# Node stages of a graph network: each close of a pass joined with the next pass's sources, and edge records laid out by partition

## The reference

```python
x = _layernorm(x + L0(x, src, dst, edge_type_16, edge_weight, ...))   # three layers
x = _layernorm(x + L1(x, edge_index, ...))
x = _layernorm(x + L2(x, edge_index, edge_attr_16, ...))
x = _layernorm(x + L3(x, node_vec, edge_weight, edge_attr_64, edge_index, ...))  # two convolutions
```

```python
ht = jnp.einsum('nd,rdo->nro', h, W_rel[l])
h_rel = segment_sum(ht[src, etype], dst) + h @ W_loop[l] + b_rel[l]
h_gat = segment_sum(softmax_over_dst(leaky_relu(el[src] + er[dst])) * z[src], dst) + b_gat[l]
hc = jnp.concatenate([h_rel, h_gat], axis=1) @ W_fuse + b_fuse      # layer 0: times a sigmoid gate
h = relu(hc)
```

## Time and profile before

| | us |
|---|---|
| median of 3 runs (lowest to highest) | 12328.44 (12322.66 to 12332.82) |
| the profiled execution | 12328.02 |
| its span, first to last instruction | 12326.2 |
| busy in it: PE / DVE / POOL / ACT | 8220.5 / 9081.5 / 6770.4 / 3431.0 |
| close and sources of L0 layer 1 together | 502.2 |
| close and sources of L0 layer 2 together | 433.0 |
| last close of L0 and sources of L1 | 375.1 |
| close of L1 and sources of L2 | 363.0 |
| close of L2 and first convolution's sources | 292.9 |
| first convolution's close, second's sources | 140.8 |
| sources of L0 layer 0 / last close | 327.0 / 99.5 |
| reading of the edge records | 203.0 |

### The profile page before, as it was taken

The page is one execution under the profiler, slowest core; times in us unless marked ns, Lnnn a source line. Parts: engine busy times, 40 slices in busy tenths (PEclk is TensorE's granted clock), DMA queues, the critical chain, the costliest instruction groups (busy, mean ns, idle before and its releaser), DMA issues. The chain is left out here.

```text
span 12326.2 us, 169288 instructions
## 1 busy us (share of the span) xinstructions
PE 8220.5 (67%) x50988; PEld 6605.6 (54%) x50988; DVE 9081.5 (74%) x15379; ACT 3431.0 (28%) x7929; POOL 6770.4 (55%) x7047
## 2 busy tenths in 40 slices
PE   3555067887678876788745778437773587858874
PEld 3444035665446654466634666425552577757774
DVE  8666547987469884589865777558887688858886
ACT  0111033333233332333312555313332111101111
POOL 2777106775037770277713777317773377727773
PEclk8555588887788887888866888757776789969996
DMA  4333674444464444644433888502222477747775
GB/s 188 108 110 108 142 305 140 107 108 81 171 226 107 108 105 134 262 107 108 107 40 123 267 269 268 130 26 56 55 56 26 146 262 265 262 111 263 262 264 134
DMA packets 825743, 1884.52 MB, mean 153 GB/s; under 512 B 378601, under 2 KB 437430, under 8 KB 785512
## 3 DMA queue, kind: packets, MB, share of 16 engines
q0 software_dynamic: 306624, 795.04, 26.0%
q1 hardware_dynamic: 518312, 1079.56, 24.5%
HBM read 1284.84 MB, written 589.18 MB: 152 GB/s over the span
## 5 line engine op out<-in xcount | busy, mean ns | idle before, releaser
L974 POOL DMA_INDIRECT h<-table,edges_ring x3552 | 3360.3, 946 | 1135.1 <-issue 1034.8
L974 POOL DMA_INDIRECT edges_rows<-table,edges_ring x1944 | 1859.4, 956 | 599.7 <-issue 578.1
L1149 PE MATMUL bank<-h,edges_onehot 128*128 128x260 f32 (+1 forms) x5312 | 1579.1, 457 | 176.4 <-DVE h L1306 130.2
L1149 PEld LDWEIGHTS bank<-h,edges_onehot 128*128 128x128 f32 x5312 | 1176.6, 253 | 470.1 <-DVE h L1306 234.7
L2434 POOL DMA_INDIRECT rec<-dst,slots x782 | 842.1, 1077 | 433.0 <-issue 414.4
L1260 DVE TENSOR_TENSOR_SCAN bank<-edges_fresh,edges_top,bank 4x1024 f32<-4x1024 bf16 x440 | 1026.2, 2332 | 3.3 <-PE bank L1124 3.3
L1267 DVE TENSOR_TENSOR_SCAN edges_top<-edges_fresh,bank 4x1024 f32<-4x1024 bf16 x440 | 995.0, 2261 | 0.8 <-issue 0.5
L1124 PE MATMUL bank<-ident,edges_score 128*4 128x128 f32 x3520 | 645.3, 345 | 485.4 <-DVE edges_score L1300 484.0
L962 POOL COPY edges_ring<-rel_idx 128x64 uint32<-128x64 uint32 (+1 forms) x42 | 10.3, 244 | 1611.9 <-POOLq L155 1611.8
L974 POOL DMA_INDIRECT acc<-table,edges_ring x664 | 682.4, 1028 | 247.5 <-issue 184.9
L1488 PE MATMUL bank<-edges_w_e,edge_score 128*128 128x128 f32 x3520 | 787.2, 311 | 0.0
(11 more groups left out here) (416 smaller groups left out, 19111.7 us busy)
## 6 DMA issues: line engine op xcount, KB each, us to landing
table<-x SPq DMA_DIRECT2D x154, 1040.0 KB, 8.0
edge_score<-edge_feat SPq DMA_DIRECT2D x220, 512.0 KB
edges_onehot<-onehot_d SPq DMA_DIRECT2D x220, 512.0 KB, 3.7
table<-h SPq DMA_DIRECT2D x77, 1040.0 KB, 7.9
table<-source_typed_rows SPq DMA_DIRECT2D x63, 1040.0 KB, 8.1
h<-table,edges_ring POOLq DMA_INDIRECT x3552
onehot_d<-edges_onehot SPq DMA_DIRECT2D x110, 512.0 KB, 3.6
flip_d<-edges_onehotT SPq DMA_DIRECT2D x110, 512.0 KB
```

Of the source, the lines that this page charges most:

```text
L974: pool.indirect_dma_start(out=rows[r][:, j, :], out_offset=None, in_=table, in_offset=bass.IndirectOffsetOnAxis(ap=ring[:, s * ST + j:s * ...
L1149: ins = pe.matmul(sum_b[k % 3], onehot[s][:, j, :], rows[s][:, j, A0:W], start=j == k * GT, stop=j == (k + 1) * GT - 1)
```

## The change

Every close is joined with the sources that follow it, in one stage with one list per engine; six stages replace twelve (the first sources stage and the last close stand alone), and their steps are written out instead of looped.

`relational_turn(layer)` is sources of an L0 layer, with the close of the layer before it in front. The work on step t+1 that comes before its typed rows is cut in slots 0 to 6, and slot j stands behind bin j of step t on PE, ACT and DVE. PE transposes straight from `acc`, `gat` and `h`; `cur` and `rel` are gone; the transposed tile and `z` have two buffers. `acc` is cleared step by step.

```diff
+    close, gated = layer > 0, layer == 1
...
+                def ahead(n, slot):        # PE
+                    if slot == 0 and close:
+                        hold(pe, loop_kept, n)
+                        turn(lambda j: g.acc[:, bin_at(n, j), 0:D])
+                    if slot == 1 and close:
...
+                        product(pe, g, 1, [(relT, w_fuse[:, 0, :]), (gatT, w_fuse[:, 1, :])], fuse_made)
...
+                    if slot == 5:
...
+                        product(pe, g, 1, [(curT[n % 2], w_z[:, :])], z_made)
+                        product(pe, g, 0, [(curT[n % 2], w_loop[:, :])], loop_made)
...
+                for slot in range(NB):
+                    ahead(0, slot)
+                for t in range(NSTEPS):
+                    for j in range(NB):
+                        typed_rows(t, j)
+                        if t + 1 < NSTEPS:
+                            ahead(t + 1, j)
...
+                    if slot == 6:          # DVE
+                        c.link(v.memset(g.acc[:, bins, D:D + ZW], 0.0))
```

`relational_to_gated` joins the last close of L0 with the sources of L1, `gated_to_attention` the close of L1 with the sources of L2 (its steps run from the last to the first), `attention_to_conv` the close of L2 with the first convolution's sources, `conv_to_conv` the two convolutions. Their DVE lists, one iteration each (function names of the new code):

```diff
+                for i in range(NSTEPS + 1):       # relational_to_gated, DVE
...
+                        attention(i)
...
+                        projected(i - 1)
...
+                        old_nodes(i)
...
+                        hidden(i - 1)
...
+                        keep_nodes(i)
...
+                        end_rows(i - 1)
...
+                for i in range(NSTEPS + 2):       # gated_to_attention, DVE
+                    if i >= 2:
+                        scores(i - 2)
+                    if i < NSTEPS:
+                        distance(i)
+                        gate_inputs(i)
+                    if 1 <= i <= NSTEPS:
+                        added(i - 1)
+                    if i < NSTEPS:
+                        mixed(i)
+                    if 1 <= i <= NSTEPS:
+                        keep_nodes(i - 1)
...
+                for i in range(NSTEPS + 2):       # attention_to_conv, DVE
+                    if i < NSTEPS:
+                        attention(i)
...
+                        added(i - 1)
...
+                        bent(i)
...
+                        keep_nodes(i - 1)
+                    if i >= 2:
+                        s.take(v, c, i - 2)
...
+                for t in range(NSTEPS):           # conv_to_conv, DVE
+                    if t + 1 < NSTEPS:
+                        close(t + 1)
+                    s.take(v, c, t)
```

The last close has two buffers for `y` and `stat`, runs a step's first half ahead of the step before's last multiplication, and its output goes out step by step:

```diff
+                for t in range(NSTEPS):           # conv_close, SP
+                    sp.wait_ge(result_ready, t + 1)
...
+                    sp.dma_start(g.out[at:at + full * P, :].rearrange("(b p) c -> p b c", p=P),
+                                 g.x[:, t * NB:t * NB + full, :]).then_inc(written, 16)
```

```diff
-                        v.tensor_tensor(slots[s][:, 0:T], rank[:, 0:T], twins[:, 0:T], ALU.add).then_inc(found_taken, 1)
+                        c.link(v.tensor_tensor(slot_i[:, 0:T], rank[:, 0:T], twins[:, 0:T], ALU.add))
+                        c.link(v.tensor_scalar(tile_i[:, 0:T], slot_i[:, 0:T], 7, None, ALU.arith_shift_right))
...
+                        v.scalar_tensor_tensor(slots[s][:, 0:T], within[:, 0:T], float(NTILES), tile_i[:, 0:T],
+                                               ALU.mult, ALU.add).then_inc(found_taken, 1)
...
-            rv = rec.rearrange("(t p) r -> p t r", p=P)
+            rv = rec.rearrange("(p t) r -> p t r", p=P)
...
+                        act.activation(places[:, at], r[:, :, PLACE], ACT.Copy)
+                        act.activation(rel_t[:, at], r[:, :, WEIGHT], ACT.Copy).then_inc(copied, 1)
...
-                        v.tensor_scalar(places[:, at], r[:, :, PLACE], 1.0, None, ALU.mult)
-                        v.tensor_scalar(rel_t[:, at], r[:, :, WEIGHT], 1.0, None, ALU.mult)
```

More of the change, by code:

```diff
@@ L322, in _ @@
[L322 to L331 removed]
+                sp.dma_start(w_z[:, :], a["L0_gnn_W_gat"][layer]).then_inc(loaded, 16)
@@ new lines, in _, with bin_range, turn_over @@
+                for slot in range(NB):
+                    ahead(0, slot)
+                for t in range(NSTEPS):
+                    for j in range(NB):
+                        typed_rows(t, j)
+                        if t + 1 < NSTEPS:
+                            ahead(t + 1, j)
+def bin_range(t):
+    return slice(t * NB, (t + 1) * NB)
+def turn_over(pe, g, bank, tiles, flipped):
+    for j in range(NB):
+        ins = pe.transpose(g.bank[bank][:, j * D:(j + 1) * D], tiles[:, j, :], g.ident[:, :])
+    ins.then_inc(flipped, 1)
@@ new lines, in keep_turned, with centre @@
+def keep_turned(act, g, bank, tile, kept):
+    act.activation(flat(tile), g.bank[bank][:, 0:NB * D], ACT.Copy).then_inc(kept, 1)
+def centre(v, c, tile, square, stat, variance_ready):
+    mean = stat[:, 0, :].unsqueeze(2).to_broadcast([P, NB, D])
+    c.link(v.tensor_reduce(stat[:, 0, :], tile[:, :, :], AX, ALU.add))
+    c.link(v.tensor_scalar(stat[:, 0, :], stat[:, 0, :], 1.0 / D, None, ALU.mult))
+    c.link(v.tensor_tensor(tile[:, :, :], tile[:, :, :], mean, ALU.subtract))
+    c.link(v.tensor_tensor(square[:, :, :], tile[:, :, :], tile[:, :, :], ALU.mult))
+    c.link(v.tensor_reduce(stat[:, 1, :], square[:, :, :], AX, ALU.add))
+    v.tensor_scalar(stat[:, 1, :], stat[:, 1, :], 1.0 / D, LN_EPS, ALU.mult, ALU.add).then_inc(variance_ready, 1)
@@ L886, in _, with close, keep_nodes @@
-                steps(v, NSTEPS, step)
+                c = Chain(v, chain)
+                def close(t):
+                    o = y[t % 2]
+                    attend(v, c, g, t, o[:, :, :], denom)
+                    c.link(v.tensor_tensor(o[:, :, :], o[:, :, :], g.acc[:, bin_range(t), 0:D], ALU.add))
+                    c.link(v.tensor_tensor(o[:, :, :], o[:, :, :], g.x[:, bin_range(t), :], ALU.add))
+                    centre(v, c, o, square, stat[t % 2], variance)
+                def keep_nodes(t):
+                    rescale(v, c, y[t % 2], g.x[:, bin_range(t), :], stat[t % 2], deviation_made, t + 1
+                            ).then_inc(result_ready, 1)
@@ L895, in superblocks @@
+                for i in range(NSTEPS + 1):
+                    if i < NSTEPS:
+                        close(i)
+                    if i:
+                        keep_nodes(i - 1)
 def superblocks(engine, step):
```

1131 lines of the change are left out of this document (604 added, 527 removed).

## The result

The changed kernel takes 11724.57 us (median of 3 runs, 11717.90 to 11725.45), before 12328.44: a ratio of 0.9509, 95% interval 0.9487 to 0.9531. 604 us are gone where 738 were forecast. The span of the profiled execution is 11722.3 us.

The account below looks back on a forecast made before the run. Touched stages were taken as bound by waiting inside chained steps, with floors from L0's DMA writes and elsewhere DVE's work. Nine savings sum to 738 us off 12328.02, giving 11,590 us; range 11,460 to 11,760.

Parts of the forecast that it names:

- R1: Rival, chance 0.13: joined L0 table steps stall on PE's waits between bins, a step keeps about 43.5 us; 11,721 us.
- The writes should go on: a step of 36.: Joined L0 stages: next step's chain stands between this step's bins, so writes continue; 36 us per step, before 43.78.
- The floor of 35.0: L0 stages: fourteen typed-row writes of 2.50 us each at 420 GB/s fill the DMA engines, 35.0 us per step.
- Three small operations count as nothing.: Ranking of records: three new DVE operations per chunk cost nothing, as the scatter waits for DVE only 18.6 us.
- R5: Rival, chance 0.02: scattered record writes 880 rows apart throttle POOL and the gain is gone; 12,328 us and above.
- The reading's pitch: Reading of records: two copies leave DVE for ACT, pitch per chunk falls from 4.63 to 3.75 us, 38 us saved.
- L1 to L2: Close of L1 with L2's sources: DVE sets the pace, 7.2 us wait for `z` stays; 34.5 per step, 98 us saved.
- The last close: Final stage: copy, round through ACT and loop branch go; step 11.87 to 10.2 us, output about 6, 20 us saved.
- L0 to L1: Last L0 close with L1's sources: a loop of dependences through PE, ACT, DVE; 34.5 us per step, 88 us saved.
- R4: Rival, chance 0.12: fuller lists keep PE at 2.4 GHz throughout, L1 stage 50 us less; 11,500 us.
- R2: Rival, chance 0.08: the three joined DVE stages still run each step as a chain, 210 us back; 11,800 us.
- R3: Rival, chance 0.03: writes limited to 358 GB/s when nothing else interrupts them, some 135 us in all; 11,725 us.

## Why the prediction was right, and which terms were not

The direction, the range and six of the nine terms (by their bounds) held; three steps of the working did not. That 11,724.57 lies in the range, 35 us under its high end, is owed to that end having been put to take in R1, and in part to luck: 160 us missing in L0 and the records stand against 33 us more than forecast elsewhere. R1's own 11,721 is all but the measured time, but its parts are not: its 43.5 us came near the step of one layer of three, and it had nothing on the records.

**"The writes should go on: a step of 36."** This failed in the layers with a close. The cover was counted as engine time (PE 26 us when warm), and PE was warm for the most part (a mean granted clock of 0.93), but its list is in order, and a wait for DVE or ACT between two bins stops the typed rows behind it. That is rival R1, which had 43.5 us for all three layers; it came as 47.75 and 42.65 in layers 1 and 2 and not in layer 0 (38.03). The run with an eighth of the writes shows that the engines' lists set the step of layer 1 (44.2 us without the writes) and help to set that of layer 2 (36.4); the spread order, with the same operations at 38.4, shows that it is their waits that do. Against the forecast's steps (36 in layer 0, 37 in layer 1 and, as its 5 us imply, 36.3 in layer 2) the terms were short by 6 x (47.75 − 37) + 6 x (42.65 − 36.3) = 103 us, and that of layer 0 by 6 x 2.0 = 12: 115 of the 122.

**The floor of 35.0.** It was read from 13 us of one step at 420 GB/s, and within a step the queue does run at that. Over whole steps it gives 393, and no order came under 38 us, since at each edge bins 6 and 0 share a buffer and the writes stop for some 3 us. The argument against R1, two buffers per half, overlooked that there is one at the edge.

**"Three small operations count as nothing."** They cost the whole of the records' gain, 40.7 us. R5 was right in sign only: it blamed the scattered writes, and the run that kept the operations without the layout shows that the writes are free. What I had read as cover, that the scatter waits for DVE only 18.6 us, says nothing of a POOL instruction that gets longer itself. The reading's pitch was right to 0.03 us per chunk; that the two copies on ACT have 0.34 of the gain was not separated in the working.

**What held.** L1 to L2: a step of 34.71 and a wait of 7.22, forecast 34.5 and 7.2; the later scores show that the wait was exposed by place. The working's own terms (27.2 less 2.5, plus 1.5 and 7.2) give 33.4, not 34.5. DVE's busy time was the 26.2 that they imply, and the missing 1.3 us are short idle times that no term names; that the forecast came so near is luck to that extent. The convolutions: 13.6 per step against 13.7. The last close: 9.99 against 10.2, and 5.7 us behind its last operation against 6. L0 to L1: the loop of dependences was there (three steps at once take it to 27.3, once ACT's order is mended), but its size was off, 30.75 for 34.5: PE ran at 2.4 GHz through more of the loop (the fusing product took 3.4 us in each step from the third on) and the stage's clock rose from 0.62 to 0.68. That is half of R4's gain there, without R4's sign, a clock over 0.8. R2 did not come: DVE is busy for 183.75 of 210.05 us between L2 and the convolution. R3 did not come either.

The Trainium skill's 358 GB/s (SBUF — State Buffer, "Summary: rules for kernel authors") is under what this core shows alone: 393 over four steps, 417 in a stretch of 23 us.

## What to carry to other kernels

When work of the next step is put between the pieces of this one, count what an in-order engine waits for at each place, not only its busy time: put a consumer a slot behind its producer. A join that leaves a dependent piece right behind its source keeps the wait; moving it half a step later takes it out. Small operations on one engine can lengthen another engine's instructions by their place alone, so a cost of nothing needs a look at what runs beside them. Where two buffers alternate within a step, see which one the next step begins with: with an odd number of pieces it is the one just filled.

## What the runs showed of the hardware

A scatter that POOL issues takes 0.96 us, and longer beside some wide DVE operations: until 0.79 to 0.80 us after the start of the sum over 1408 numbers, in three kernels, and 2.3 us beside the comparison that writes 128x1408 bf16 (some 64 of the 782 scatters in each). The Trainium skill (SBUF — State Buffer, "Summary: rules for kernel authors") says that POOL's writing of descriptors starves while DVE is in a fast mode. That some DVE operations hold the scatters and others beside them don't, the trace shows; in which mode they ran, it does not.

Writes of 1.065 MB each in one queue ran at 417 to 420 GB/s in stretches of 13 to 23 us and at 393 over four steps of 38 us, with a DMA share of 0.96; in the step shown, the difference lies at its edge, where the share was 0.17 for 3 us.
